# Second phase of a gated cross-attention kernel: who writes its constants and who issues the loads of its MLP weights

## The chip, the cores and the metric

The kernel runs on one core of a Trainium2 chip. The core has TensorE (PE in the profile) for matrix products, VectorE (DVE), ScalarE (ACT), GpSimd (POOL) and SyncE (SP), which issues the DMAs. The metric is the device time of one execution in microseconds; several executions are taken and their median stands for the kernel. One further execution is recorded by the profiler, and every row below comes from that one.

## The reference

The input x is 32 batches of 256 rows by 256 columns; a context of the same size and a mask of 256 by 256 per batch go with it. Four gated residual steps follow each other:

```python
x = x + jnp.tanh(g_xattn[0]) * _L0_xattn_ref(_layernorm(x, axis=-1), ctx_1024, ctx_1024, ...)
x = x + jnp.tanh(g_ffn[0]) * _L0_ffn_ref(_layernorm(x, axis=-1), L0_ffn_weight, L0_ffn_bias)
x = x + jnp.tanh(g_xattn[1]) * _L1_xattn_ref(_layernorm(x, axis=-1), ctx_1024, ctx_1024, mask_Bx1xSxS2_if1, ...)
x = x + jnp.tanh(g_ffn[1]) * _L1_ffn_ref(_layernorm(x, axis=-1), ...)
```

The first phase of the kernel computes the first line. The second line needs one scale over the whole of x (an fp8 quantisation with `quant_fp8`), so the second phase can only start when the first is through. The second phase computes the last three lines: the quantised product, an attention with 16 heads of 16 columns, and an MLP whose weights are dequantised on the chip:

```python
w = (q.astype(jnp.float32) - 128.0).reshape(K // g, g, N) * scales[:, None, :]   # g = 128
y = hf @ w1 + fc1_bias      # 256 -> 1024, then silu
z = y @ w2 + fc2_bias       # 1024 -> 256
```

## The kernel before

x stays in SBUF through both phases. The second phase, `phase_b`, is a pipeline over the 32 batches that is written out by hand for each engine. `iteration(half, parity)` is one step of it, and iteration k works on eight stages at once: n (batch k) is scaled and rounded for the fp8 product, f (batch k-1) gets the product and its update of X, q (k-2) the projections to queries, keys and values, m (k-3) the maxima of the scores, a (k-4) the exponentials and the product with V, o (k-5) the output projection, h (k-6) the first half of the MLP, w (k-7) its second half. Each engine has its own list of calls for an iteration and runs it in that order; semaphores with names (`sig["y"]`, `sig["ones_set"]`) bind the engines together. The first ten iterations and the last seven or so are written out, those between are a loop. Whether a piece of work stands in an iteration is decided by `if n:`, `if f:` and so on, and for work that happens once by `at_iteration(half, parity, k)`.

Around the change:

- Batch 0 goes through VectorE's `scaled`, `binades`, `magic` (tiles `v`, `e`), GpSimd's `rounded` (`v` at L1200, `y` at L1204), four transposing loads on SyncE (`yT<-y`, L1118), TensorE's quantised product (L1736), and VectorE's `quantised_update`: `ob` at L1471 and X at L1475. GpSimd may write `y` of the next batch only when the loads of the last have landed.
- Constants are written once by GpSimd at the end of its iteration 0: 1.0 into both buffers of V (whose columns 16 to 31 of each head sum the exponentials), 0.0 into `nm` (the maxima, of which the transposing load also takes columns that nobody fills), 1.0 into both buffers of K4 (the stacked keys, of which one row multiplies the row of maxima). Five increments of `ones_set` tell the others.
- The tiles Y and YT of the MLP, 1 MB each, also serve as the landing place of the quantised weights and their scales: `load_weights` puts the integers into Y and the scales, repeated over the partitions, into YT. SyncE issues this for fc1 at the end of iteration 0 and for fc2 at the end of iteration 4, then behind waits for `f1lo` and `b1_mm`, which say that fc1 has been taken out.
- VectorE dequantises fc1 at the end of iteration 2 (L1424, L1426), ScalarE and VectorE split it into a bf16 part and a rest in iteration 3 (`f1`), and TensorE multiplies YT with the beta column (`first_bias`, L1671) there. fc2 goes the same way at the end of iteration 5 (`f2`).
- On SyncE iteration 4 ends with the transposed maxima (L1127) and the row of maxima that is laid into Q4 (L1135). TensorE's first transposed score of iteration 5 waits for that row, and ScalarE's first exponential of iteration 5 for this score.
- `load_functions` is a table load of ScalarE, two in every iteration (L31).

Of the kernel before, what the change touches and what calls it, by code (L numbers as in the profile page):

```python
# [6 lines left out]
ALU = mybir.AluOpType  # L7
# [4 lines left out]
P = 128  # L12
D = 256
C = D // P
# [909 lines left out]
def phase_b(nc, a, NB, out_d, ctxT_d, mask_d, X, mu1, rsq, scale_qk, gate, ident, identb, minus_half, f1, f2, b1f, any_masked,  # L924
# [15 lines left out]
    with scope:  # L940
# [227 lines left out]
        def _(pool):  # L1168
# [6 lines left out]
            def iteration(half, parity):  # L1175
# [99 lines left out]
        def _(act):  # L1275
            def iteration(half, parity):
# [70 lines left out]

                if q:
                    normalised_high()
# [33 lines left out]

                if at_iteration(half, parity, 3):

                    act.wait_ge(sig["w1"], 1)
                    for c in range(C):
                        last = nc.scalar.activation(f1[:, 0, c], whole_YT[:, c * HID:(c + 1) * HID], ACT.Copy,
                                                    scale=second["g_col"][:, c:c + 1])
                    last.then_inc(sig["f1hi"], 1)  # L1390
                if at_iteration(half, parity, 5):

                    act.wait_ge(sig["w2"], 1)
                    nc.scalar.activation(f2[:, 0].rearrange("p h d -> p (h d)"), whole_YT, ACT.Copy).then_inc(sig["f2hi"], 1)

# [3 lines left out]
        def _(dve):  # L1399
# [28 lines left out]
            def iteration(half, parity):  # L1428
# [138 lines left out]
                if at_iteration(half, parity, 4):  # L1567

                    dve.wait_ge(sig["b1_mm"], 1)
                    nc.vector.tensor_tensor(b1f[:, :], second["b1_raw"][:, :], b1_ps, ALU.add).then_inc(sig["b1f"], 1)  # L1570
                if h:
                    mlp_normalised()
# [48 lines left out]

                if at_iteration(half, parity, 2):
                    dequantised("f1_in", "w1")
                if at_iteration(half, parity, 3):

                    dve.wait_ge(sig["f1hi"], 1)
                    for c in range(C):
                        last = nc.vector.scalar_tensor_tensor(f1[:, 1, c], whole_YT[:, c * HID:(c + 1) * HID],
                                                              second["g_col"][:, c:c + 1], f1[:, 0, c], ALU.mult,
                                                              ALU.subtract)  # L1630
                    last.then_inc(sig["f1lo"], 1)
# [304 lines left out]
```

## Time and profile before

| what | us |
|---|---|
| median of 3 runs | 1703.47 |
| lowest and highest | 1703.34, 1705.59 |
| the profiled execution | 1701.08 |
| its span, first to last instruction | 1699.2 |
| TensorE busy in it | 1555.5 (92%) |
| VectorE busy | 1369.5 (81%) |
| ScalarE busy | 1045.2 (62%) |
| GpSimd busy | 941.0 (55%) |

Times in the trace are counted from the start of the span. The second phase starts at about 675; its filling lasts until about 830, the loop and its ends from there. A row of the timeline gives the start, the length, the engine, the line of the kernel, the operation and its tiles; in brackets stands how long the engine had been idle before it and what ended that. Rows that follow each other in equal form are merged, with their count. Busy shares are means over stages with different limits, so a place is judged by the chain of work there and not by the share.

### The profile page before, as it was taken

To read this page: it belongs to the slowest core of one execution; us is meant where nothing else is said; L and a number is where in the kernel's file an instruction comes from. 1 tells how busy PE (TensorE), PEld (TensorE's weight loads), DVE (VectorE), ACT (ScalarE), POOL (GpSimd) and SP (SyncE) were. 2 spreads that over 40 slices of the span, in tenths; PEclk is the share of its full clock that TensorE was granted. 3 is DMA by queue.
4 is the path that set the end of the run, shared out by engine and by line. 5 is a ranking of instruction groups with operands and counts; after the bars stand their busy time and mean duration, and the time that the engine had idled before them with its cause. 6 is when DMAs were issued, how large, how long until landed. Compare 5 with 4: busy or idle time off the path is not lost.

```text
span 1699.2 us, 40740 instructions
## 1 busy us (share of the span) xinstructions
PE 1555.5 (92%) x13387; PEld 1206.5 (71%) x13387; DVE 1369.5 (81%) x3213; ACT 1045.2 (62%) x1894; POOL 941.0 (55%) x1328
## 2 busy tenths in 40 slices
PE   5999999999999995376999999999999999999987
PEld 4888888888888884243667766676767676767666
DVE  5688888888888776777899989899888988898743
ACT  6666666666666654245666666666665657575654
POOL 4555556665566534424465656565655656564535
PEclk9999999999999998568999999999999999999999
DMA  7312221222221100323222323232232322222100
GB/s 217 103 63 62 73 82 62 62 62 64 86 66 62 37 1 29 92 81 115 76 82 76 90 73 87 71 86 77 78 85 74 88 74 82 80 80 81 56 16 20
DMA packets 197687, 125.40 MB, mean 74 GB/s; under 512 B 44400, under 2 KB 196848, under 8 KB 197360
## 3 DMA queue, kind: packets, MB, share of 16 engines
q1 hardware_dynamic: 197616, 124.48, 25.0%
q8 instruction: 42, 0.69, 0.2%
q14 instruction: 29, 0.24, 0.0%
HBM read 92.69 MB, written 25.17 MB: 69 GB/s over the span
## 4 chain that ended last, share of the span: by engine, by line
PE 38%; ACT 7%; issue 5%; DVE 3%; SPq 3%; DMA 2%; POOL 1%; ACTq 0%; POOLq 0%
PE b_bank L1646 22%; PE b_bank L1721 6%; PE b_scoreT L1703 4%; PE b_score L1686 3%; ACT L31 2%; ACT b_E L1284 2%; ACT b_Y L1344 2%; PE b_bank L1654 1%; DMA b_nmT<-b_nm 1%; DVE b_nm L1466 1%; PE b_bank L1736 1%; ACT b_xT L1290 1%; DMA b_Q<-b_nmT 1%; SPq L1102 1%; SPq L1091 1%
## 5 line engine op out<-in xcount | busy, mean ns | idle before, releaser
L1466 DVE TENSOR_REDUCE b_nm<-b_score 128x4 bf16<-128x1024 f32 x256 | 314.3, 1228 | 73.4 <-PE b_score L1686 73.2
L1284 ACT ACTIVATE b_E<-b_scoreT 128x1024 f32<-128x1024 f32 x256 | 262.5, 1025 | 156.0 <-PE b_scoreT L1703 155.6
L760 PE MATMUL bank<-W2T,G 128*128 128x256 f32 x1024 | 231.2, 379 | 0.0
L1213 POOL TENSOR_SCALAR b_YT<-b_Y 128x512 bf16<-128x512 f32 x128 | 85.7, 669 | 248.5 <-ACT b_Y L1344 240.2
L760 PEld LDWEIGHTS bank<-W2T,G 128*128 128x128 f32 x1024 | 192.1, 190 | 24.8
L31 ACT ACT_TABLE_LOAD x156 | 200.1, 1283 | 9.7 <-PEq L875 6.4
L1344 ACT ACTIVATE b_Y<-b_bank,b1f 128x256 f32<-128x256 f32 x256 | 107.3, 470 | 158.8 <-PE b_bank L1646 158.4
L1646 PE MATMUL b_bank<-b_hT,f 128*128 128x256 bf16 x1536 | 188.7, 273 | 11.2 <-ACT b_Y L1344 10.9
L1646 PE MATMUL b_bank<-f,b_YT 128*128 128x256 bf16 x1536 | 183.5, 273 | 2.5 <-POOL b_YT L1216 1.6
L727 PE MATMUL bank<-hT,W1T 128*128 128x256 bf16 x1536 | 178.3, 273 | 6.2 <-ACT G L497 2.5
L1646 PEld LDWEIGHTS b_bank<-b_hT,f 128*128 128x128 bf16 x1536 | 142.8, 98 | 54.0 <-ACT b_Y L1344 19.2
L727 PEld LDWEIGHTS bank<-hT,W1T 128*128 128x128 bf16 x1536 | 147.8, 98 | 34.6 <-ACT G L497 15.9
L1646 PEld LDWEIGHTS b_bank<-f,b_YT 128*128 128x128 bf16 x1536 | 145.1, 98 | 31.9 <-issue 12.9
L1216 POOL TENSOR_TENSOR b_YT<-b_Y,b_YT 128x512 bf16<-128x512 f32 x128 | 148.0, 1156 | 10.7
L1721 PE MATMUL b_bank<-b_E,b_V 128*32 128x256 f32 x2048 | 132.5, 388 | 0.0
L497 ACT ACTIVATE G<-bank,b1c 128x256 f32<-128x256 f32 x256 | 103.2, 466 | 46.0 <-PE bank L727 46.0
L1703 PE MATMUL b_scoreT<-b_Q,b_K 49*128 49x256 bf16 x1024 | 101.2, 276 | 28.4 <-ACT b_E L1284 18.7
L1686 PE MATMUL b_score<-b_K,b_Q 48*128 48x256 bf16 x1024 | 101.4, 277 | 16.7 <-DVE b_nm L1466 15.6
L1721 PEld LDWEIGHTS b_bank<-b_E,b_V 128*32 128x32 f32 x2048 | 57.3, 110 | 49.4 <-issue 22.6
L346 POOL TENSOR_SCALAR ve<-mv 128x2 f32<-128x2 f32 x32 | 6.9, 215 | 148.5 <-issue 143.5
L454 ACT ACTIVATE E<-bank,low 128x256 f32<-128x256 f32 x64 | 29.7, 469 | 93.9 <-DVE low L569 93.9
L1703 PEld LDWEIGHTS b_scoreT<-b_Q,b_K 49*128 49x128 bf16 x1024 | 33.3, 95 | 74.9 <-ACT b_E L1284 29.5
(206 smaller groups left out, 3378.9 us busy)
## 6 DMA issues: line engine op xcount, KB each, us to landing
b_Q<-q_dram SPq DMA_DIRECT2D x192, 64.0 KB, 2.5
b_K<-k_dram SPq DMA_DIRECT2D x192, 64.0 KB, 2.5
xin<-in_x SPq DMA_DIRECT2D x32, 256.0 KB, 4.3
ctxn<-in_ctx SPq DMA_DIRECT2D x32, 256.0 KB, 2.8
mask_in<-in_mask SPq DMA_DIRECT2D x32, 256.0 KB, 3.0
X<-in_x SPq DMA_DIRECT2D x32, 256.0 KB, 4.1
ctxt<-in_ctxT SPq DMA_DIRECT2D x32, 256.0 KB, 4.4
b_ctxt<-in_ctxT SPq DMA_DIRECT2D x32, 256.0 KB, 2.8
```

The lines of the kernel that those rows point to most:

```text
L31: act.add_instruction(mybir.InstLoadActFuncSet(name=nc.get_next_instruction_name(), act_func_set_id=which, ins=[], outs=[]))
L497: last = nc.scalar.activation(G[m.parity][:, 2 * j + i], mlp_ps[j % 2][:, i], ACT.Gelu, bias=b1c[:, 2 * j + i:2 * j + i + 1])
L727: last = nc.tensor.matmul(out_tile, lhs(i, k), rhs(j, k), start=k == 0 and (i, j) == TERMS[0], stop=k == chunks[-1] and (i, j) == TERMS[-1])
L760: last = nc.tensor.matmul(out_ps[:, t], G[w.parity][:, h, t * P:(t + 1) * P], W2T[:, h], start=h == 0, stop=h == HC - 1)
L1216: nc.gpsimd.tensor_tensor(YT[:, 1, 2 * j:2 * j + 2], Y[:, 2 * j:2 * j + 2], YT[:, 0, 2 * j:2 * j + 2], ALU.subtract).then_inc(sig["Ylo"], 1)
L1284: nc.scalar.activation(E[:, pair:pair + 2], scoreT_ps[:, :, :, :], ACT.Exp).then_inc(sig["E"], 1)
L1344: last = nc.scalar.activation(Y[:, 2 * j + i], bank[BANK[f"H{j}"]][:, i], ACT.Silu, bias=b1f[:, 2 * j + i:2 * j + i + 1])
L1466: nc.vector.tensor_reduce(pair, score_ps[:, :, :, :], AX.X, ALU.max, negate=True).then_inc(sig["nm"], 1)
L1646: last = nc.tensor.matmul(out_tile, lhs(i, k), rhs(j, k), start=start and k == chunks[0] and (i, j) == TERMS[0], stop=stop and k == chunks ...
L1686: last = nc.tensor.matmul(score_ps[:, odd, t], Q4[m.parity][rows, i, tile(t)], K4[m.parity][rows, i, :], start=True, stop=not mask)
L1703: last = nc.tensor.matmul(scoreT_ps[:, odd, k], K4[a.parity][rows, i, tile(k)], Q4[a.parity][rows, i, :], start=True, stop=not mask)
L1721: last = nc.tensor.matmul(bank[BANK[name]][ONE * j:ONE * (j + 1), g % 2, :], V[a.parity][:, k, i, :], E[:, i % RING, k, :], start=k == 0, ...
```

## The change

GpSimd no longer writes the constants; ScalarE writes them at the end of its iteration 0 with ACTIVATE Copy (input times 0.0 plus the value, `ident` as an input of one column that is repeated). `load_weights` moves from SyncE to ScalarE, for fc1 behind those constants, for fc2 at the end of ScalarE's iteration 4 behind the same two waits. The splitting of `f1` and `f2` on ScalarE and VectorE is put into functions (`weights_high`, `weights_low`) and called at the same places; `first_bias` asks for its iteration itself.

```diff
         @block.sync
         def _(sp):
-            def load_weights(ints, layout, rows, scales, step):
-                sp.dma_start(whole_Y.bitcast(I32).rearrange("p (c o) -> p c o", c=rows),
-                             a[ints].rearrange(layout, p=P)).then_inc(sig[step], 16)
-                sp.dma_start(whole_YT, a[scales].to_broadcast([P, HC * S])).then_inc(sig[step], 16)
-
...
-                if at_iteration(half, parity, 0):
-                    load_weights("fc1_q", "(c p) o -> p c o", C, "fc1_scales", "f1_in")
-                if at_iteration(half, parity, 4):
-
-                    sp.wait_ge(sig["f1lo"], 1)
-                    sp.wait_ge(sig["b1_mm"], 1)
-                    load_weights("fc2_q", "(c p) o -> p c o", HC, "fc2_scales", "f2_in")
...
-                if at_iteration(half, parity, 0):
-                    nc.gpsimd.memset(V[0][:, :, :, :], 1.0).then_inc(sig["ones_set"], 1)
-                    nc.gpsimd.memset(V[1][:, :, :, :], 1.0).then_inc(sig["ones_set"], 1)
-                    nc.gpsimd.memset(nm[:, :, :], 0.0).then_inc(sig["ones_set"], 1)
-                    for i in range(2):
-                        nc.gpsimd.memset(K4[i][:, :, :], 1.0).then_inc(sig["ones_set"], 1)
...
         @block.scalar
         def _(act):
+            def load_weights(ints, layout, rows, scales, step):
+                act.dma_start(whole_Y.bitcast(I32).rearrange("p (c o) -> p c o", c=rows),
+                             a[ints].rearrange(layout, p=P)).then_inc(sig[step], 16)
+                act.dma_start(whole_YT, a[scales].to_broadcast([P, HC * S])).then_inc(sig[step], 16)
...
+                def weights_high():
+                    if at_iteration(half, parity, 0):
+                        for tensor, value in ((V[0], 1.0), (V[1], 1.0), (nm, 0.0), (K4[0], 1.0), (K4[1], 1.0)):
+                            whole = tensor.ap()
+                            nc.scalar.activation(whole, ident[:, 0:1].to_broadcast(list(whole.shape)), ACT.Copy, scale=0.0,
+                                                 bias=value).then_inc(sig["ones_set"], 1)
+                        load_weights("fc1_q", "(c p) o -> p c o", C, "fc1_scales", "f1_in")
...
+                    if at_iteration(half, parity, 4):
+
+                        act.wait_ge(sig["f1lo"], 1)
+                        act.wait_ge(sig["b1_mm"], 1)
+                        load_weights("fc2_q", "(c p) o -> p c o", HC, "fc2_scales", "f2_in")
```

How the instructions stand now, at the places that matter. GpSimd at the start of the second phase, before (two additions for batch 0, the constants, two for batch 1):

```order
L1173 MEMSET b_pool_fence 128x64
L1200 TENSOR_TENSOR b_v<-b_v,b_e 128x512
L1204 TENSOR_TENSOR b_y<-b_v,b_e 128x512
L1266 MEMSET b_V_0 128x1024
L1267 MEMSET b_V_1 128x1024
L1268 MEMSET b_nm 128x256
L1270 MEMSET b_K4_0 128x2048
L1270 MEMSET b_K4_1 128x2048
L1200 TENSOR_TENSOR b_v<-b_v,b_e 128x512
L1204 TENSOR_TENSOR b_y<-b_v,b_e 128x512
```

GpSimd there with the change:

```order
L1159 MEMSET b_pool_fence 128x64
L1186 TENSOR_TENSOR b_v<-b_v,b_e 128x512
L1190 TENSOR_TENSOR b_y<-b_v,b_e 128x512
L1186 TENSOR_TENSOR b_v<-b_v,b_e 128x512
L1190 TENSOR_TENSOR b_y<-b_v,b_e 128x512
```

The five memsets are gone from between the two batches. ScalarE at the same start, before (the table loads of iterations 0 and 1, then iteration 2):

```order
L31 ACT_TABLE_LOAD x4
L1290 ACTIVATE b_xT<-b_bank9 128x512
L31 ACT_TABLE_LOAD
L1303 ACTIVATE b_qs<-b_bank8,bq_col 128x256 x2
L1311 ACTIVATE b_ks<-b_bank6,bk_col 128x256 x2
```

ScalarE there with the change:

```order
L1335 ACTIVATE b_K4_0<-ident 128x2048
L1335 ACTIVATE b_K4_1<-ident 128x2048
L1255 DMA b_Y<-in_fc1_q 128x2x1024
L1257 DMA b_YT<-in_fc1_scales 128x2048
L31 ACT_TABLE_LOAD x2
L1273 ACTIVATE b_xT<-b_bank9 128x512
```

The fills (of which the last two are shown) and the two loads of fc1 now stand between the second and the third table load. SyncE at the end of iteration 4 and the start of iteration 5, before:

```order
L1127 DMA_TRANSPOSE b_nmT_1<-b_nm 128x128 x2
L1135 DMA b_Q4_1<-b_nmT_1 1x8x256 x2
L1051 DMA b_Y<-in_fc2_q 128x8x256
L1053 DMA b_YT<-in_fc2_scales 128x2048
L1062 DMA b_ctxt<-in_ctxT 128x2x256
L1069 DMA b_mask_in<-in_mask 128x2x256
L1118 DMA_TRANSPOSE b_yT<-b_y 128x128 x4
```

ScalarE at the same place with the change (exponentials of iteration 4, its copies, then iteration 5):

```order
L31 ACT_TABLE_LOAD
L1307 ACTIVATE b_oS<-b_bank9 128x512
L1316 ACTIVATE b_V_0<-b_bank6 128x16x16 x2
L1255 DMA b_Y<-in_fc2_q 128x8x256
L1257 DMA b_YT<-in_fc2_scales 128x2048
L1273 ACTIVATE b_xT<-b_bank9 128x512
L31 ACT_TABLE_LOAD
```

The two loads of fc2 have gone from behind the row of maxima on SyncE to between the copies of V and of xT on ScalarE.

## Rows read from the trace of the kernel before

**Rows 1.** stages: PE, PEld, DVE, ACT, POOL busy; clock, DMA share, GB/s

```profile
686.00:709.00 23.00, 8.67 (x48) 5.80 (x48) 14.51 (x33) 5.50 (x9) 10.40 (x12) 0.65 0.27 77
...
860.00:1610.00 750.00, 727.24 (x7706) 522.12 (x7706) 662.81 (x1283) 483.14 (x755) 442.55 (x569) 1.00 0.28 79
```

**Rows 2.** the chain that ended last, 683 to 690: start, length, what

```profile
683.53 2.38 DMA b_yT<-b_y
...
687.95 1.84 DVE X L1475
```

**Rows 3.** line L1475: shortest/median/longest ns, all batches

```profile
L1475 DVE SCALAR_TENSOR_TENSOR X<-b_ob,gate,X x32: 750/752/1844, 687.9 to 1563.0; 128x512 bf16 x22, 128x512 f32<-128x512 bf16 x10
```

**Rows 4.** timeline of GpSimd, start of the second phase

```profile
681.62 3.55 POOL L1270 MEMSET b_K<- 128x2048 bf16 x2
686.64 1.27 POOL L1200 TENSOR_TENSOR b_v<-b_v,b_e 128x512 f32<-128x512 f32 x1 [1.47 <-DVE b_e L1547]
687.98 1.26 POOL L1204 TENSOR_TENSOR b_y<-b_v,b_e 128x512 bf16<-128x512 f32 x1
```

**Rows 5.** timeline of VectorE: v of batches 1 and 2, dequantising fc1

```profile
679.68 5.95 DVE L1529 TENSOR_SCALAR b_v<-X,mu,rsq 128x256 f32<-128x256 f32 x2 [2.79 <-POOL b_y L1204]
...
694.09 0.73 DVE L1529 TENSOR_SCALAR b_v<-X,mu,rsq 128x256 f32<-128x256 f32 x2
...
709.12 1.75 DVE L1424 TENSOR_SCALAR b_Y<-b_Y 128x2048 f32<-128x2048 int32 x1
```

**Rows 6.** the chain that ended last, 762 to 770

```profile
763.59 2.36 DMA b_nmT<-b_nm
...
766.78 1.75 DMA b_Q<-b_nmT
```

**Rows 7.** timeline of ScalarE, iteration 4 to 5

```profile
766.13 0.66 ACT L1333 ACTIVATE b_V<-b_bank 128x256 f32<-128x256 f32 x2 [1.64 <-PE b_bank L1646]
766.67 0.61 ACT L1290 ACTIVATE b_xT<-b_bank 128x512 bf16<-128x512 f32 x1
767.29 1.28 ACT L31 ACT_TABLE_LOAD   x1
769.01 1.02 ACT L1284 ACTIVATE b_E<-b_scoreT 128x1024 f32<-128x1024 f32 x1 [0.43 <-PE b_scoreT L1703]
```

**Rows 8.** timeline of SyncE's queue: fc1, transposing loads, fc2

```profile
675.60 0.46 SPq L1053 DMA_DIRECT2D b_YT<-in_fc_scales  x1
...
679.75 5.02 SPq L1118 DMA_TRANSPOSE b_yT<-b_y  x4
...
767.52 0.41 SPq L1051 DMA_DIRECT2D b_Y<-in_fc_q  x1
767.97 1.54 SPq L1053 DMA_DIRECT2D b_YT<-in_fc_scales  x1
```

**Rows 9.** timeline of ScalarE: start of the second phase, and f2

```profile
675.19 5.15 ACT L31 ACT_TABLE_LOAD   x4 [6.41 <-PEq L875]
695.44 0.60 ACT L1290 ACTIVATE b_xT<-b_bank 128x512 bf16<-128x512 f32 x1 [15.10 <-PE b_bank L1654]
...
791.71 1.91 ACT L1394 ACTIVATE f<-b_YT 128x2048 bf16<-128x2048 f32 x1 [3.49 <-DVE b_YT L1426]
```

**Rows 10.** landings: scales; L1118 768 to 780; L1118 675 to 700

```profile
DMA to landing us min/median/max: 7.0/7.4/7.8
...
DMA to landing us min/median/max: 4.2/5.7/7.3
...
DMA to landing us min/median/max: 2.3/2.4/3.9
```

**Rows 11.** timeline of TensorE: twelve matmuls, slow and fast; b1 product

```profile
696.82 2.74 PE L1646 MATMUL b_bank<-b_xT,wqkvo 128*128 128x256 bf16 x12 [1.42 <-DVE b_xT L1433]
...
703.32 1.48 PE L1646 MATMUL b_bank<-wqkvo,b_cT 128*128 128x256 bf16 x12 [1.40 <-DVE b_ks L1504]
...
733.41 6.83 PE L1671 MATMUL b_scoreT<-b_col,b_YT 128*128 128x1 f32 x32
```

More of the change, by code:

```diff
@@ L1346, in silu @@
                     last.then_inc(sig["Y"], 1)
+                def weights_high():
[5 more added lines that the diff above has]
+                        load_weights("fc1_q", "(c p) o -> p c o", C, "fc1_scales", "f1_in")
+                    if at_iteration(half, parity, 3):
+                        act.wait_ge(sig["w1"], 1)
+                        for c in range(C):
+                            last = nc.scalar.activation(f1[:, 0, c], whole_YT[:, c * HID:(c + 1) * HID], ACT.Copy,
+                                                        scale=second["g_col"][:, c:c + 1])
+                        last.then_inc(sig["f1hi"], 1)
+                    if at_iteration(half, parity, 5):
+                        act.wait_ge(sig["w2"], 1)
+                        nc.scalar.activation(f2[:, 0].rearrange("p h d -> p (h d)"), whole_YT, ACT.Copy).then_inc(sig["f2hi"], 1)
+                    if at_iteration(half, parity, 4):
+                        act.wait_ge(sig["f1lo"], 1)
+                        act.wait_ge(sig["b1_mm"], 1)
+                        load_weights("fc2_q", "(c p) o -> p c o", HC, "fc2_scales", "f2_in")
                 if q:
@@ L1382, in iteration @@
                     silu(3)
[L1384 to L1394, printed above, removed]
+                weights_high()
             pipeline(act, iteration, NB, LAGS)
@@ L1570, in iteration, with weights_low @@
                     nc.vector.tensor_tensor(b1f[:, :], second["b1_raw"][:, :], b1_ps, ALU.add).then_inc(sig["b1f"], 1)
+                def weights_low():
+                    if at_iteration(half, parity, 2):
+                        dequantised("f1_in", "w1")
+                    if at_iteration(half, parity, 3):
+                        dve.wait_ge(sig["f1hi"], 1)
+                        for c in range(C):
+                            last = nc.vector.scalar_tensor_tensor(f1[:, 1, c], whole_YT[:, c * HID:(c + 1) * HID],
+                                                                  second["g_col"][:, c:c + 1], f1[:, 0, c], ALU.mult,
+                                                                  ALU.subtract)
+                        last.then_inc(sig["f1lo"], 1)
+                    if at_iteration(half, parity, 5):
+                        dequantised("f2_in", "w2")
+                        dve.wait_ge(sig["f2hi"], 1)
+                        nc.vector.tensor_tensor(f2[:, 1].rearrange("p h d -> p (h d)"), whole_YT,
+                                                f2[:, 0].rearrange("p h d -> p (h d)"), ALU.subtract).then_inc(sig["f2lo"], 1)
                 if h:
@@ L1620, in iteration @@
                     base()
[L1622 to L1631, printed above, removed]
-                if at_iteration(half, parity, 5):
-                    dequantised("f2_in", "w2")
-                    dve.wait_ge(sig["f2hi"], 1)
-                    nc.vector.tensor_tensor(f2[:, 1].rearrange("p h d -> p (h d)"), whole_YT,
-                                            f2[:, 0].rearrange("p h d -> p (h d)"), ALU.subtract).then_inc(sig["f2lo"], 1)
+                weights_low()
             pipeline(dve, iteration, NB, LAGS)
@@ L1666, in first_bias @@
                 def first_bias():
+                    if not at_iteration(half, parity, 3):
+                        return
                     pe.wait_ge(sig["w1"], 1)
@@ L1882, in iteration @@
                     hidden(3)
-                if at_iteration(half, parity, 3):
-                    first_bias()
+                first_bias()
             some = pe.value_load(any_masked[0:1, 0:1], min_val=0, max_val=1)
```

## The prediction, as it was put on record

> **What bounds the kernel now.** I read the view by stages first. In the 750 us from 860 to 1610 TensorE is busy for 727.24 us at full clock; in the 23 us from 686 to 709, in which the second phase starts, it is busy for 8.67 us, at 0.65 of full clock [rows 1]. The change touches nothing in the stage that repeats. Its instructions all stand in iterations 0 and 4 of the filling, written out ahead of the loop. So nothing is multiplied by 32, and what it can be worth is read from the chain that ended last, at two places.
>
> First place, the chain from 683 to 690 [rows 2]: the fourth transposing load of y for batch 0 takes from 683.53 to 685.91, TensorE makes the quantised product, VectorE `ob`, and then VectorE takes 1.84 us for X at L1475, from 687.95. That last row is strange: over all 32 batches the same line takes 0.750 at least, 0.752 in the median and 1.844 at most [rows 3]. The reader is to see why in GpSimd's rows [rows 4]. Right behind y of batch 0 stand five memsets, of which the last two take 3.55 us from 681.62, up to 685.17. VectorE's `v` for batch 1, issued at 679.68, stays open for 5.95 us [rows 5], until 685.63, and GpSimd's additions for batch 1, which wait for VectorE, run at 686.64 and 687.98, about 1.26 us each, so that the second lies on top of the 1.84 us instruction. The striking 5.95 us are not on the chain: what is late there is the transposing load.
>
> Second place, the chain from 762 to 769: transposed maxima (2.36 us of DMA), the row of maxima laid into Q4 (1.75 us of DMA), the transposed scores, and ScalarE's first exponential of iteration 5 at 769.01 [rows 6, 7]. The load of fc2 is issued behind this, at 767.52 [rows 8].
>
> **The change part by part.**
>
> *Constants leave GpSimd.* The five memsets go. `v` of batch 1 is done some 5.2 us sooner (5.95 against the 0.73 us of batch 2 [rows 5]). GpSimd's `v` addition follows at about 681.3. Its `y` addition has to wait until `yT` of batch 0 has landed, 685.91 [rows 2], and so ends at about 687.2. `ob` hangs on TensorE's product and X starts at 687.95 as before: by then GpSimd is idle, waiting for VectorE's statistics. Term A is 1.84 - 0.75 = **-1.09 us**, on the chain. What comes behind (statistics, GpSimd's power, `xh`, TensorE's transposes, ScalarE's copy) is one chain in which each waits for the one before, so the whole filling moves by that much. The ends of this term are 0 and -1.09.
>
> *Constants go to ScalarE.* It loads four tables from 675.19 for 5.15 us and then does nothing until 695.44, idle for 15.10 us [rows 9]. The new work stands between the second and the third table load. A fill of 128x2048 to bf16 goes by the nearest row, 1.91 us for f2 [rows 9]: two of these, two of half the size, one of an eighth, together 2 x 1.91 + 2 x 0.96 + 0.24 = about 6 us. ScalarE is free again at about 675.2 + 5.15 + 6 = 686.3, plus 0.9 us of issue, 687.2, against a need at about 694.4 (695.44 less term A). That costs nothing; it begins to cost if the fills take over twice as long. Those who wait for the constants (SyncE before it stacks the keys of batch 0, ScalarE itself before V, VectorE before its first maximum, behind the row at 709.12 [rows 5]) come more than 10 us later. Also nothing.
>
> *The load of fc1 moves.* It is 2 MB; on SyncE its second half is issued at 675.60 in 0.46 us and lands 7.0 to 7.8 us after its issue [rows 8, 10]. VectorE takes it at 709.12 [rows 5]. Even issued behind the fills, at 683.8, it lands by 692. Hidden, with 17 us to spare. But it may fall on the transposing loads of `yT` (issued from 679.75 for 5.02 us [rows 8]), and those are on the chain. Of the eight such loads from 675 to 700 the median lands after 2.4 us and the slowest, beside the burst of fc1 itself, after 3.9 us; behind the burst of fc2 they take 4.2 to 7.3 us [rows 10]. Term B lies between 0 and 7.3 - 2.4 = +4.9 us. I take **0**: if ScalarE issues it early, the burst ends near 683.4 as it does now; if it issues it behind the fills, at 683.8, three of the four loads are through. Only a start between 679 and 682 is bad.
>
> *The load of fc2 moves.* SyncE is rid of 0.41 + 1.54 us at 767.52 [rows 8]; its next loads start up to 1.95 us sooner and nobody is waiting for them. ScalarE gets the two issues between the copy of V (766.13, for which it had been idle 1.64 us) and the copy of `xT` at 766.67, behind which stand a table load (767.29 to 768.57) and the exponential at 769.01 [rows 7]. No row shows an issue from ScalarE; the nearest are SyncE's. If it comes in its turn, ScalarE loses 1.95 us, of which the 0.44 us between the table and the exponential cover a part: +1.51 us on the chain, through TensorE's second transposed score and all that follows it. If the queue issues it while the engine waits for V, it is covered but for 1.95 - 1.64 = 0.31 us. Term C is 0 to +1.51; I take **+0.31**, because the later of the two waits in front of the issue, `b1_mm`, was met at 740.24 [rows 11], and ahead of it stands only work of the engine that waits for TensorE. The page that bears on this is in the Trainium skill, Perfetto Trace Analysis, "Per-engine timelines": an instruction of ScalarE goes to a wait queue and the sequencer decodes on. By it term C would be 0 or 0.31, and fc1 would be issued as early as now. No run here shows it.
>
> VectorE's and TensorE's edits only put the same instructions into functions; their order stays.
>
> **The sum.** -1.09 + 0 + 0 + 0.31 = -0.78 us. The profiled execution took 1701.08 us (span 1699.2): it would take 1700.3. That execution lies 2.39 us below the median of the three runs; the difference is carried over to the median: 1703.47 - 0.78 = **1702.7 us**. The 0.2% that a measurement of this kernel can tell from no change is 3.4 us.
>
> **The rivals.**
>
> *In its turn* (chance 0.2). ScalarE issues fc2 only behind V: -1.09 + 1.51 = +0.4, 1703.9 us. For it: order in the program. Against it: nothing that the trace can show.
>
> *The burst falls on the chain* (0.18), the one that ends slower. If ScalarE's queue can issue fc2 while the engine waits, the 2 MB start two or more us sooner, beside the transposed maxima and the row of maxima (2.36 and 1.75 us [rows 6]). Beside a burst the same kind of transfer took 1.8 to 4.9 us more. That gives -1.09 + 1.8 = +0.7 up to -1.09 + 4.9 = +3.8, 1704.2 to 1707.3 us. It is slower than before as soon as the delay exceeds 1.1 us, and measurably slower from 4.5 us. Against it: in [rows 10] the loads stood behind the burst in one queue, here they would be in two. The rule against the change is in the Trainium skill, DMA: Bandwidth & Descriptors, "Issuing engines are not separate DMA queues": a DMA issued from ScalarE runs on the same 16 engines and interleaves, and only issue time is saved. By that the move gains nothing and a delay above 0 is to be expected. The same mechanism at term B has the same prices.
>
> *The change doesn't relieve the chain* (0.1). The 1.84 us of L1475 has another cause than GpSimd, or `yT` lands so that GpSimd's `y` falls on it again: A is 0, 1703.5 to 1704.3 us. The one length in 32 and the overlap speak against it.
>
> *TensorE's clock shifts* (0.12). From 686 to 709 it is granted 0.65 of full speed [rows 1]; twelve matmuls take 2.74 us at 1.2 GHz and 1.48 us at 2.4 GHz, both on this path [rows 11]. A shift of all work by 1 us can move a few such groups from one level to the other: 1.26 us each, one to three of them, either way: 1699 to 1707 us.
>
> **How the numbers follow.** The forecast has 0.4. Its own range is -1.4 to +0.5 around the median. The range for 8 in 10 takes in the rival in its turn, most of the burst, one or two groups of matmuls and what executions of one kernel differ by (2.39 us down, 2.12 us up): 1700.6 to 1706.5. Faster by over 0.2% would take two or three groups at the better clock besides term A: 0.05, all from the clock. Slower by over 0.2% needs the burst near its upper end (0.04) or the clock (0.02). Within: 0.89.
>
> **What would show it.** Right: L1475's longest is near 0.75 us; `v` of batch 1 takes 0.7 us; ScalarE's issues of fc2 leave `xT` on time; all marks of the filling up to 766 are 1.1 us earlier. Wrong: `yT` or the row of maxima land later; a gap of 2 us on ScalarE at the end of iteration 4; another clock in 686 to 740.

## The result and the profile after

The changed kernel takes 1713.26 us in the median (1707.32 to 1715.89, five runs), the kernel before beside it 1704.52 (1703.34 to 1705.59, five runs). The ratio is 1.0049, with a 95% interval of 1.0028 to 1.0071: slower by some 0.5%, where 1702.7 (1700.6 to 1706.5) had been forecast. The profiled execution of the changed kernel took 1707.32 us (span 1705.5), that of before 1701.08 (span 1699.2), so the two traces show 6.3 us of the difference.

The stage that repeats is the same (727.74 us of TensorE against 727.24 in [rows 1]). The stages of the filling are not. Stages of the changed kernel, columns as in [rows 1]:

```profile
686.00:709.00 23.00, 8.76 (x48) 5.87 (x48) 13.19 (x32) 5.72 (x10) 9.42 (x12) 0.65 0.27 78
...
740.00:772.00 32.00, 21.27 (x184) 10.80 (x183) 20.76 (x38) 16.32 (x21) 6.77 (x8) 0.76 0.36 109
...
860.00:1610.00 750.00, 727.74 (x7705) 522.96 (x7703) 663.95 (x1283) 483.48 (x758) 443.51 (x569) 1.00 0.28 80
```

To find where the time went I take marks in both traces, relative to VectorE's first instruction of the second phase (675.23 before, 675.19 after):

| mark, us from the start of the phase | before | after | difference |
|---|---|---|---|
| TensorE's quantised product of batch 0 | 10.73 | 11.52 | +0.79 |
| X of batch 0 starts | 12.72 | 13.50 | +0.78 |
| VectorE's `xT` of batch 0 (L1433 before) | 20.84 | 20.54 | -0.30 |
| TensorE's b1 product | 58.18 | 57.96 | -0.22 |
| first transposed score of iteration 5 | 93.35 | 97.88 | +4.53 |
| TensorE's transposes of `hn` | 122.19 | 128.82 | +6.63 |
| first result of the phase | 175.40 | 181.89 | +6.49 |
| end of the span | 1023.97 | 1030.31 | +6.34 |

The loss arises between the b1 product and the transposes of `hn` and stays to the end.

**First place.** The chain that ended last, changed kernel, 683 to 690, answering to [rows 2] (start, length, what):

```profile
683.49 3.17 DMA b_yT<-b_y
...
688.69 0.75 DVE X L1470
```

X takes 0.75 us, as forecast, and the longest of the 32 is now 753 ns, where [rows 3] had 1844. But `yT` lands 3.17 us after its last issue instead of 2.38. ScalarE's timeline in the changed kernel shows why (ACT is the engine, ACTq its queue, which issues the DMAs); it answers to [rows 9] and to the first row of [rows 8]:

```profile
675.15 2.57 ACT L31 ACT_TABLE_LOAD   x2 [6.41 <-PEq L875]
677.73 1.05 ACT L1335 ACTIVATE b_V<-ident 128x1024 f32<-128x1024 f32 x1
677.74 0.45 ACTq L1255 DMA_DIRECT2D b_Y<-in_fc_q  x1
678.23 0.48 ACTq L1257 DMA_DIRECT2D b_YT<-in_fc_scales  x1
...
679.94 3.69 ACT L1335 ACTIVATE b_K<-ident 128x2048 bf16<-128x2048 f32 x2
683.65 2.57 ACT L31 ACT_TABLE_LOAD   x2
```

In the program the load of fc1 stands behind the five fills. The queue issues it at 677.74, when the engine has just begun the first of them, but not ahead of the two table loads, which end at 677.72. So the 2 MB start 2.6 us later than before and are still moving when the transposing loads go out.

**Second place.** ScalarE from iteration 4 to 5 in the changed kernel, answering to [rows 7]:

```profile
765.89 0.38 ACT L1316 ACTIVATE b_V<-b_bank 128x256 f32<-128x256 f32 x1 [1.64 <-PE b_bank L1642]
765.96 0.39 ACTq L1255 DMA_DIRECT2D b_Y<-in_fc_q  x1
...
766.37 0.61 ACTq L1257 DMA_DIRECT2D b_YT<-in_fc_scales  x1
767.08 0.60 ACT L1273 ACTIVATE b_xT<-b_bank 128x512 bf16<-128x512 f32 x1 [0.53 <-issue]
...
773.72 1.02 ACT L1267 ACTIVATE b_E<-b_scoreT 128x1024 f32<-128x1024 f32 x1 [4.74 <-PE b_scoreT L1700]
```

The issue itself is cheap: two instructions, 0.39 and 0.61 us, and ScalarE waits 0.53 us for its queue ahead of `xT`, at 767.08 against 766.67. The queue issued fc2 0.07 us after the first copy of V had begun (765.89); it did not do so in the 1.64 us for which the engine had waited for that copy. The exponential comes 4.71 us later (773.72 against 769.01) for another reason, which the chain that ended last shows, answering to [rows 6]:

```profile
764.08 2.38 DMA b_nmT<-b_nm
...
767.29 5.73 DMA b_Q<-b_nmT
...
773.07 0.63 PE b_scoreT L1700 x3
```

SyncE's row of maxima, two pieces of 4 KB, takes 5.73 us from its issue where it took 1.75. fc2 was issued 0.6 us ahead of it (765.96 against 766.55), by another queue, where SyncE had issued it 1.5 us behind it (767.52 against 766.04, [rows 8]). TensorE's rows, and its granted clock in steps of 1 us, both of the changed kernel:

```profile
773.07 0.60 PE L1700 MATMUL b_scoreT<-b_Q,b_K 49*128 49x256 bf16 x4 [5.48 <-DMA b_Q<-b_nmT]
...
775.76 2.74 PE L1642 MATMUL b_bank<-b_xT,wqkvo 128*128 128x256 bf16 x12
...
780.52 1.48 PE L1642 MATMUL b_bank<-b_cT,wqkvo 128*128 128x256 bf16 x12
```

```profile
771.00:772.00 1.00, 0.00 (x0) 0.00 (x0) 0.00 (x0) 0.00 (x0) 0.00 (x0) 1.00 1.01 417
772.00:773.00 1.00, 0.00 (x0) 0.00 (x0) 0.00 (x0) 0.00 (x0) 0.00 (x0) 0.56 1.01 413
773.00:774.00 1.00, 0.93 (x6) 0.53 (x7) 0.00 (x0) 0.28 (x1) 0.00 (x0) 0.50 0.91 321
```

TensorE stands still for 5.48 us; in the gap its clock falls from full speed to half of it (2.4 to 1.2 GHz), while the DMA engines move over 400 GB/s. The twelve matmuls that follow take 2.74 us; in the kernel before the same twelve took 1.48, at 770.64. The loss adds up: the row was issued 0.55 us later (the first transposing load of the maxima took SyncE 1.84 us against 1.11), it travelled 3.98 us longer, together 4.53; and by 780.52 the half clock had added another 2.1 (+6.64 there; 105.33 against 98.69 us from the start of the phase).

### The profile page after: what moved, and what is told of

Read it like the earlier page. It is cut to its first block, busy times and chain, and to the rows that moved or that the text cites. A ratio compares the mean times of both kernels' runs of the same rounds, so it can differ in the third digit from the quotient of the medians.

```text
span 1705.5 us, 40740 instructions
## 1 busy us (share of the span) xinstructions
PE 1557.9 (91%) x13387; PEld 1207.2 (71%) x13387; DVE 1362.1 (80%) x3213; ACT 1051.1 (62%) x1899; POOL 935.7 (55%) x1323
## 4 chain that ended last, share of the span: by engine, by line
PE 38%; ACT 7%; issue 5%; DVE 4%; DMA 3%; SPq 2%; POOL 1%; ACTq 0%; POOLq 0%
PE b_bank L1642 22%; PE b_bank L1718 6%; PE b_scoreT L1700 4%; PE b_score L1683 3%; ACT L31 2%; ACT b_E L1267 2%; ACT b_Y L1327 2%; DVE b_nm L1461 1%; PE b_bank L1650 1%; DMA b_nmT<-b_nm 1%; DMA b_Q<-b_nmT 1%; PE b_bank L1733 1%; ACT b_xT L1273 1%; SPq L1122 1%; SPq L1097 1%
```

## The experiments

The theory after the result: fc2, started ahead of the row of maxima by another queue, holds the row up (some 4 us), and the gap costs TensorE its clock (some 2 us more). Rivals: ScalarE's time is the cost; the load of fc1 or the constants are; the traffic slows all work beside it. The mark that tells most is the first result of the phase, since what comes after differs between executions of one kernel (below). "Late" is counted against the profiled execution of before, from the start of the phase; each kernel has one profile, the change two.

**Only fc2 back on SyncE.** From the changed kernel:

```diff
 # SyncE, end of iteration 4
+                if at_iteration(half, parity, 4):
+                    sp.wait_ge(sig["f1lo"], 1)
+                    sp.wait_ge(sig["b1_mm"], 1)
+                    load_weights("fc2_q", "(c p) o -> p c o", HC, "fc2_scales", "f2_in")
 # ScalarE, weights_high
-                    if at_iteration(half, parity, 4):
-                        act.wait_ge(sig["f1lo"], 1)
-                        act.wait_ge(sig["b1_mm"], 1)
-                        load_weights("fc2_q", "(c p) o -> p c o", HC, "fc2_scales", "f2_in")
```

> The change with the load of fc2 back at the end of SyncE's iteration 4; constants and fc1 stay on ScalarE. Theory (the 2 MB of fc2, issued from ScalarE ahead of the row of maxima, hold that row for 5.73 instead of 1.75 us, and TensorE's clock falls in the gap): the row lands after 1.75 us again and the time is that of before, from 1.1 us less (L1475) to 0.8 us more (yT beside fc1), in the profile about 0.3 us less. Rival (the constants and fc1 at the start, which shift all work and so the clock, make the loss): still 6 to 9 us slower than before.

Measured: 1703.13 us against 1704.26, ratio 0.9993 (0.9980 to 1.0006). The row of maxima takes 1.75 us again, the first result is 0.4 us late. In its chain at the start `yT` and X read much as in the changed kernel:

```profile
681.86 3.06 DMA b_yT<-b_y
...
686.95 0.75 DVE X L1475
```

So the whole measurable loss goes with the place of fc2. The load of fc1 on ScalarE's queue costs 0.7 us at the landing of `yT` and the constants give 1.09 back.

**Only fc2 on ScalarE,** everything else as in the kernel before:

```diff
 # SyncE, end of iteration 4: the block with load_weights of fc2 is gone
 # ScalarE, end of iteration 4
+                if at_iteration(half, parity, 4):
+                    act.wait_ge(sig["f1lo"], 1)
+                    act.wait_ge(sig["b1_mm"], 1)
+                    load_weights("fc2_q", "(c p) o -> p c o", HC, "fc2_scales", "f2_in")
```

> The kernel before with only the load of fc2 moved, to the end of ScalarE's iteration 4. Theory (burst on the row of maxima): 6 to 9 us slower than before, the row lands after 5 us or more, VectorE's L1475 keeps its 1.84 us. Rival (the loss needs the constants and fc1): within 1.5 us of before.

Measured: 1708.64 us, ratio 1.0024 (1.0009 to 1.0039). The start of the phase is that of before, X at L1475's place keeps its 1.84 us, and the row of maxima is held up as in the change:

```profile
766.08 5.70 DMA b_Q<-b_nmT
...
771.83 0.63 PE b_scoreT L1708 x4
```

The first transposed score is 5.04 us late, the first result 6.32. One part alone makes the loss of the filling. Its median is 4.4 us above that of before, less than the 6 to 9 us expected.

**Only the constants on ScalarE.** Both loads stay on SyncE; the ACTIVATEs of the change write the constants.

```diff
 # GpSimd, end of iteration 0: the five memsets are gone
 # ScalarE, weights_high
+                    if at_iteration(half, parity, 0):
+                        for tensor, value in ((V[0], 1.0), (V[1], 1.0), (nm, 0.0), (K4[0], 1.0), (K4[1], 1.0)):
+                            whole = tensor.ap()
+                            nc.scalar.activation(whole, ident[:, 0:1].to_broadcast(list(whole.shape)), ACT.Copy, scale=0.0,
+                                                 bias=value).then_inc(sig["ones_set"], 1)
```

> Only the constants on ScalarE, both loads on SyncE. Term A by itself: 1.1 us less than before in the profile, X of batch 0 in 0.75 us, yT of batch 0 landed 2.4 us after its issue as before; in the times 0 to 1.1 us less, which is inside what executions differ by. Rival: as slow as the change.

Measured: 1703.68 us, ratio 0.9999 (0.9981 to 1.0017). At the start of its second phase the chain reads:

```profile
681.77 2.39 DMA b_yT<-b_y
...
686.19 0.75 DVE X L1476
```

`xT` of batch 0 comes at 19.75 us, 1.09 sooner than before: term A to the hundredth. At the b1 product 0.20 of it is left, and the profiled execution as a whole is not 1.1 us shorter, as had been expected, but as long as that of before (1701.22 against 1701.08). TensorE's rows of iteration 2, first of this kernel and then of the kernel before:

```profile
693.97 2.74 PE L1648 MATMUL b_bank<-b_xT,wqkvo 128*128 128x256 bf16 x12 [1.41 <-DVE b_xT L1434]
696.50 2.57 PE L1648 MATMUL b_bank<-b_cT,wqkvo 128*128 128x256 bf16 x12
```

```profile
699.35 2.13 PE L1646 MATMUL b_bank<-b_cT,wqkvo 128*128 128x256 bf16 x12
```

The first twelve take 2.74 in both [rows 11]; of the second twelve, fewer run at the full clock when the work comes sooner, 2.57 against 2.13. Counted from the start of the phase the second twelve start at 23.0 us here and at 24.1 in the kernel before, but the clock rises at 25.3 and at 25.4. From 709 to 740 the mean granted clock is 0.56 in this kernel and 0.61 in the kernel before. The work came sooner, the time at which the clock stood at its higher level hardly did. The two groups account for 0.44 of the 0.89 us lost by the b1 product; the rest was not followed.

**The change again,** unaltered, beside these.

> The change, unaltered, again. Its five executions went from 1707 to 1716 us and the profiled one was the fastest. Theory: executions differ in how much of the burst stands ahead of the row and in how long TensorE is slow after the gap; 3 to 12 us above before, at a mean granted clock lower the slower they are, and the row of maxima late in each profile. Rival (one odd first series): all within 1 us of before.

Measured: 1711.94 us (twelve runs), ratio 1.0040 (1.0027 to 1.0052). Row of maxima 5.87 us, first result 6.43 late. In more executions the result stands; the two shortest had a mean granted clock of 0.968, the longest 0.962.

**fc2 on ScalarE, but behind the row.** From the changed kernel: the four lines of fc2 go out of `weights_high` and stand between the two first exponentials of iteration 5.

```diff
                 if a:
                     exponential(0)
+                if at_iteration(half, parity, 5):
+                    act.wait_ge(sig["f1lo"], 1)
+                    act.wait_ge(sig["b1_mm"], 1)
+                    load_weights("fc2_q", "(c p) o -> p c o", HC, "fc2_scales", "f2_in")
+                if a:
                     exponential(1)
```

> The change with the load of fc2 still issued by ScalarE, but behind the first exponential of iteration 5, which cannot start before the row of maxima has landed. Theory (what costs is the place of the burst ahead of the row, not the queue that issues it): the row lands 1.75 us after its issue, the first transposed score of iteration 5 comes about 94 us after the start of the second phase as in the kernel before (93.35) and with fc2 on SyncE (94.20), and the time is within 2 us of before. Rival (an issue or a burst from ScalarE's queue costs wherever it stands): 4 us or more above before, ScalarE's second exponential late by 1 us or more.

Measured: 1705.52 us against 1702.74, ratio 1.0016 (0.9998 to 1.0034). ScalarE's timeline:

```profile
770.83 1.02 ACT L1267 ACTIVATE b_E<-b_scoreT 128x1024 f32<-128x1024 f32 x1 [1.48 <-PE b_scoreT L1700]
770.89 0.42 ACTq L1255 DMA_DIRECT2D b_Y<-in_fc_q  x1
771.34 0.64 ACTq L1257 DMA_DIRECT2D b_YT<-in_fc_scales  x1
772.34 1.03 ACT L1267 ACTIVATE b_E<-b_scoreT 128x1024 f32<-128x1024 f32 x1 [0.49 <-PE b_scoreT L1700]
```

The two issues lie under the first exponential, and the next one waits for TensorE, as it does before. The first transposed score is 0.32 us late, the first result 0.11 early. The same queue, engine and bytes cost nothing here: the loss is neither ScalarE's time nor ScalarE's queue, it is the order. The median is 2.8 us above the one of before, where at most 2 had been expected, with an interval that just takes in 1; the filling doesn't show these 2.8, so this stays open.

**fc2 ahead of the row, but on SyncE.** From the kernel before; ScalarE has no part in it.

```diff
 # SyncE, end of iteration 4
                     transpose_maxima()
+                    if at_iteration(half, parity, 4):
+                        sp.wait_ge(sig["f1lo"], 1)
+                        sp.wait_ge(sig["b1_mm"], 1)
+                        load_weights("fc2_q", "(c p) o -> p c o", HC, "fc2_scales", "f2_in")
                     row_of_maxima()
 # ... and the block behind it is gone
```

> The kernel before with the load of fc2 on SyncE, but between the transposed maxima and the row of maxima. Theory (the row stands behind the burst in the DMA engines, whichever queue issued it): the row lands 5 us or more after its issue, TensorE's first transposed score of iteration 5 is 4 to 6 us late, the whole 5 to 12 us slower. Rival (only a second queue disturbs the first): the row lands after 1.75 us, the time is that of before.

Measured: 1713.52 us (one run). Row of maxima on the chain:

```profile
766.41 6.34 DMA b_Q<-b_nmT
...
772.80 0.63 PE b_scoreT L1702 x3
```

Here with one queue 6.34 us, there with two 5.70 to 5.87. First result 6.98 late. But here fc2 had a longer start on the row (issued at 764.41, the row at 765.68, so 1.27 us against 0.59 to 1.05). Counted from the issue of fc2 the row lands after 8.34 us here and after 7.06 to 7.49 with two queues; here 0.4 us behind the scales of fc2, there 0.8 to 1.2 ahead of them. A second queue saves the row 0.9 to 1.3 us of the wait behind 2 MB, not the wait. This is one profile of the one-queue kernel.

**Half of fc2 ahead of the row.** From the kernel before, 1 MB on ScalarE at the end of iteration 4, the other half on SyncE behind the row: once the integers, once the scales.

```diff
 # the one with the integers on ScalarE
+                if at_iteration(half, parity, 4):
+                    act.wait_ge(sig["f1lo"], 1)
+                    act.wait_ge(sig["b1_mm"], 1)
+                    act.dma_start(whole_Y.bitcast(I32).rearrange("p (c o) -> p c o", c=HC),
+                                 tensors["fc2_q"].rearrange("(c p) o -> p c o", p=P)).then_inc(sig["f2_in"], 16)
 # SyncE, in the place of load_weights
+                    sp.dma_start(whole_YT, tensors["fc2_scales"].to_broadcast([P, HC * S])).then_inc(sig["f2_in"], 16)
```

> The kernel before, with the integers of fc2 (1 MB) issued by ScalarE at the end of iteration 4 and the scales (1 MB) by SyncE behind the row of maxima. Theory (the row waits for what is queued ahead of it): about half of the delay, the row lands 3 to 4.5 us after its issue instead of 5.7, the first transposed score of iteration 5 at 95 to 97 us after the start of the phase. Rival (any issue from ScalarE costs the same): 5.7 us as with both halves.

> As the run before, the halves exchanged: the scales (1 MB, one row of 8 KB repeated over the partitions) from ScalarE, the integers from SyncE behind the row. Theory (bytes ahead count): again 3 to 4.5 us. If the form of the transfer counts (long rows against 1 KB pieces), the two halves differ by over 1 us.

Measured: 1710.74 and 1707.32 us (one run each). The row of maxima on the two chains, first with the integers ahead, then with the scales:

```profile
767.01 4.48 DMA b_Q<-b_nmT
```

```profile
764.50 4.18 DMA b_Q<-b_nmT
```

Against 1.75 that is 2.73 and 2.43 us more for 1 MB, 3.95 to 4.12 for 2 MB on the second queue. The rearranged integers and the repeated scales differ little. The other half was issued 0.7 us behind the row, while the row was still moving; what it added isn't separated. With one issue in place of two ScalarE's `xT` is not delayed (0.60 and 0.55 us behind V, 0.54 before). Half the bytes don't save half of the loss: the first result is 6.55 and 5.71 us late. That asked for an experiment in which the row is late and nothing is in its way.

**A late row without traffic.** The kernel before; SyncE counts up a semaphore that nobody waits for, 40 or 80 times, between the landing of the maxima and the issue of their row, in iteration 4 alone. All loads keep queue and order.

```diff
+                    if at_iteration(half, parity, 4):
+                        for _ in range(40):          # 80 in the second
+                            sp.sem_inc(sig["row_late"], 1)
                     sp.sem_inc(sig["row_ready"], 1)
```

> The kernel before with SyncE made to count up a semaphore that nobody waits for 40 times between the landing of the maxima and the issue of the row of them, in iteration 4 alone; all loads in their old places and queues, so no burst stands ahead of the row. It asks what a late row costs without the traffic. At 0.05 us for each count (the steps between two issues of SyncE in the trace of before are 0.04 to 0.06 us) the row is issued 2 us later. Theory (only the lateness of the row costs, and what is beyond it is TensorE's clock after the longer gap): row 1.75 us from issue to landing, first transposed score 2 us later, and the first result by more than that, 3 to 6 us, as in the run with the scales alone on ScalarE's queue (2.3 us late, 5.7 us at the first result). Rival (the traffic beside the work costs the rest): the first result is late by the same 2 us or less.

> The same with 80 counts, the row issued 4 us later, as late as it landed in the changed kernel. Theory: row 1.75 us from issue to landing, first transposed score 4 to 5 us later, TensorE's clock falls in the gap as in the changed kernel, and the first result is 6 to 7 us late, the time 1709 to 1713. Rival (the burst itself slows the work): the first result is late by 4 us or less, the time 1706 to 1708. A third one: SyncE's loads behind the row (fc2, the context and the transposing loads of batch 1) go out 4 us later too, and cost something of their own; then yT of batch 1 is what ends the wait for the next MLP, and the loss is over 7 us.

Measured: with 40 counts 1712.46 us (one run), with 80 counts 1710.29 us (ten runs), ratio 1.0030 (1.0014 to 1.0047). Chain and stages of the kernel with 40:

```profile
771.84 1.76 DMA b_Q<-b_nmT
...
773.64 0.63 PE b_scoreT L1706 x3
```

```profile
768.00:772.00 4.00, 0.98 (x8) 0.54 (x8) 2.84 (x5) 1.75 (x2) 2.79 (x4) 1.00 0.01 2
772.00:776.00 4.00, 2.29 (x16) 1.28 (x16) 0.64 (x3) 1.02 (x1) 0.00 (x0) 0.69 0.50 152
```

The DMA engines move next to nothing (2 GB/s) from 768 to 772, the row needs its 1.76 us, and the clock falls to half all the same (0.50 from 774 to 775, behind a wait of 4.63 us that ended at 773.64). The row went out later than I had put (3.10 and 5.82 us, for 2 and 4): the counts took some 2.9 and 5.2 us, and in both kernels the transposing load of the maxima took SyncE 2.1 us instead of 1.11. The first result is 6.15 and 7.18 us late, as in the kernels with a burst. The rival in which traffic slows the work beside it falls. The third one had a loss of over 7 us as its sign, and 7.18 just meets it; but the late row accounts for it as in the others (5.84 at the score, 1.42 added by the transposes of `hn`, nothing after), and up to the first result TensorE's longer waits are for the same work as in the changed kernel.

Put together, lateness of the first transposed score of iteration 5, of the transposes of `hn` and of the first result, one profile each:

| kernel | score late | `hn` late | first result late |
|---|---|---|---|
| only the constants | -0.19 | -0.19 | -0.56 |
| fc2 on ScalarE behind the row | 0.32 | 0.50 | -0.11 |
| fc2 back on SyncE | 0.85 | 0.85 | 0.41 |
| fc1 first on ScalarE (below) | 1.22 | 2.78 | 2.90 |
| scales ahead | 2.31 | 3.81 | 5.71 |
| 40 counts | 3.12 | 5.60 | 6.15 |
| integers ahead | 3.75 | 6.29 | 6.55 |
| the change | 4.53 | 6.63 | 6.49 |
| the change again | 4.82 | 6.80 | 6.43 |
| only fc2 on ScalarE | 5.04 | 6.95 | 6.32 |
| fc2 ahead, on SyncE | 5.55 | 7.26 | 6.98 |
| 80 counts | 5.84 | 7.26 | 7.18 |

In the first three kernels the clock stays at full speed around the first scores of iteration 5, and by `hn` at most 0.2 us is added to the lateness (in two of them it falls for some 3 us about 12 us later, at no cost that this mark shows). In the other nine profiles it falls to half in the gap or just behind it, for 3 to 7 us, and 1.4 to 2.5 us are added. So the price is the lateness itself plus some 2 us for the clock, and the second part hardly depends on the first. The last column flattens for another reason too: with the scales ahead another 1.9 us are lost behind `hn`, where the clock is at half again (0.50 from 832 to 834, 1.00 there in the kernel before); why isn't shown.

**fc1 first on ScalarE,** the version meant to keep the gain: constants on ScalarE, fc2 on SyncE at its old place, fc1 issued by ScalarE as the first thing of its iteration 0, ahead of the table loads.

```diff
+                if at_iteration(half, parity, 0):
+                    load_weights("fc1_q", "(c p) o -> p c o", C, "fc1_scales", "f1_in")
                 if q:
                     normalised_high()
```

> The version meant to keep the gain and drop the losses: the constants stay on ScalarE, fc1 is issued by ScalarE as the first thing of its iteration 0, ahead of its table loads and fills, and fc2 goes back to the end of SyncE's iteration 4. Theory (fc1 costs only where it overtakes the transposing loads of batch 0, and fc2 only where it overtakes the row of maxima): yT of batch 0 depends on how far ahead of it fc1 starts. In the change fc1 started 2.5 us behind the start of the phase and yT took 3.17 us; before, it was issued behind yT and yT took 2.38. Started at the very beginning, the 2 MB have moved for most of their 7 us by the time yT is issued, so 2.4 to 4 us for yT; row of maxima 1.75 us; first result within 1 us of the kernel before; time 1702 to 1705 against 1704.3 of before, not to be told from it. Rival (a load on a second queue always delays the chain that runs beside it, and an earlier start only moves the place): yT is 1 to 4 us later than before, and the end 1 to 4 us later, 1705 to 1708.

Measured: 1704.11 us against 1704.58, ratio 0.9997 (0.9981 to 1.0014). ScalarE and the chain at the start of the phase:

```profile
675.71 0.46 ACTq L1265 DMA_DIRECT2D b_Y<-in_fc_q  x1
676.21 0.48 ACTq L1267 DMA_DIRECT2D b_YT<-in_fc_scales  x1
676.72 2.57 ACT L31 ACT_TABLE_LOAD   x2 [7.42 <-issue]
```

```profile
684.06 2.40 DMA b_yT<-b_y
...
688.49 0.75 DVE X L1476
```

Issued 2 us sooner than in the change, fc1 is out of the way, and `yT` lands after 2.40 us. (The expectation has it that the kernel before issued fc1 behind `yT`; [rows 8] has it at 675.6 and `yT` at 679.75. This version gives fc1 its old moment back, so it does not test an earlier one.) `xT` of batch 0 comes 1.06 sooner, and again nothing of it reaches the end. Its profiled execution happened to be a long one (1712.24): the transposing load of the maxima took SyncE 2.41 us instead of 1.11, which made the row 1.22 late with no load near it, and the result 2.90, where within 1 had been expected. TensorE's clock fell behind this wait too, to 0.50 from 773 to 774; its rows show the wait and the twelve matmuls behind it, which took 1.48 us in the kernel before:

```profile
770.32 0.39 PE L1706 MATMUL b_scoreT<-b_Q,b_K 49*128 49x256 bf16 x4 [2.06 <-DMA b_Q<-b_nmT]
...
772.38 2.36 PE L1648 MATMUL b_bank<-b_xT,wqkvo 128*128 128x256 bf16 x12
```

None of the kernels beats the one before by an amount that can be told.

## Why the prediction was wrong, point by point

**What bounds the kernel now** held: the repeating stage is untouched, and the two places that I read were the two that moved.

**Term A (-1.09)** was right in mechanism and size where it acts (X 0.75, `xT` of batch 0 at -1.09 with the constants alone). Wrong was "the whole filling moves by that much": by the b1 product 0.20 was left, and about half of what was lost is seen in slower matmuls. It was a gain of a start, in a stretch in which the clock sets how long TensorE's part takes. The fills took 5.9 us (677.73 to 683.63) against 6 forecast, hidden as argued.

**Term B (0)** fell between the two ends: +0.7 to +0.8. I reasoned "if ScalarE issues it early, the burst ends near 683.4 as it does now". The queue passed the fills but not the table loads, so early meant 2.6 us later than before, and the burst ended near 685.5. I had written that only a start between 679 and 682 is bad; one at 677.7 was enough.

**Term C (+0.31) is the step that failed.** In the sum it priced the *issue* and put the *transfer* at nothing. The price of the issue came out near (`xT` 0.41 us later in the trace, 0.65 us later behind V: 1.19 against 0.54), but partly by luck. I had the two issues take 1.95 us and hide in the 1.64 us for which the engine waits for V; they took 1.00 us, came only after that wait, and hid in part under the copies. The sentence "the later of the two waits in front of the issue was met at 740.24" said already that fc2 would leave as soon as ScalarE's queue got to it, at about 766.0, 1.5 us sooner than before and so ahead of the row of maxima instead of behind it. From there it follows from [rows 10]: loads behind the burst of fc2 had landed after 4.2 to 7.3 us. The true term was +3.98 for the row, inside the 1.8 to 4.9 of the rival, and that rival, which had 0.18, is what happened. The argument against it, two queues instead of one, was worth about 1 us: in two queues the row landed 7.06 to 7.49 us after the issue of fc2, in one 8.34. The Trainium skill, DMA: Bandwidth & Descriptors, "Issuing engines are not separate DMA queues", says that DMAs of different engines interleave on the same 16 engines; the runs agree with it, and I should have given it the weight of the sum and not of a rival.

**The clock rival (0.12) and the burst rival were not rivals** but one case. I had the clock as noise that comes "either way" from a shift of 1 us; what it did was follow from a gap of 5.5 us, and add 2.1 us. Lateness of the score 4.53 (the 0.2 left of term A is in it), clock 2.1: 6.6, which is what the profile gives at the transposes of `hn` (6.63; 6.49 at the first result). That GpSimd is not the cause of the 1.84 us is refuted by the rows. fc2 in its turn is refuted in its price (+1.51) and half so in its mechanism: the issue waited with the first copy of V and then went ahead of the second.

**The range** ended at 1706.5 since it took in most of the burst without its follow-up; slower by over 0.2%, which is what came, had 0.06. With the follow-up, the burst's case is 1703.47 + 0.7 to + 3.8, and 2 for the clock: 1706 to 1709. The measured medians, 1711.94 and 1713.26, are higher still, 7.7 and 8.7 us above those of before. What is left beside the 6.4 of the filling, 1.3 and 2.3 us, has no profile that shows its place. The emptying is the likely one, since there executions differ: from the first result to the end of the span the kernel before took 848.6 us in its profile, the kernel with the constants alone 851.1, the change 848.4 and then 854.2, while to X of the last batch it was 712.4 to 713.4 us in all four. From 1640 to 1660, kernel before, and then only fc2 on ScalarE:

```profile
1640.00:1660.00 20.00, 18.71 (x188) 13.68 (x188) 7.12 (x19) 12.44 (x19) 8.40 (x12) 1.00 0.05 15
```

```profile
1640.00:1660.00 20.00, 17.75 (x134) 10.23 (x133) 1.74 (x6) 9.98 (x11) 0.65 (x1) 0.66 0.01 2
```

TensorE is busy for about as long but does 134 matmuls for 188, at 0.66 of its clock. Whether the change makes this more frequent was not settled; single executions of before range from 1697 to 1711 us. Nor was it settled why the whole change is 3.3 us slower in the median than fc2 alone (the intervals, 1.0027 to 1.0052 and 1.0009 to 1.0039, overlap, and the fillings agree within 0.1 us).

## What to carry to other kernels

When a load is moved to another engine's queue, don't price the issue; ask at what moment the queue reaches it now, which small transfer is issued right behind that moment, and who waits for that one. If the answer is TensorE, and the gap grows past what it bridged before, add a clock that falls, here some 2 us. And a gain at the start of a filling is only worth what is left of it once TensorE's clock has risen: read it at a late mark, not where it arises.

## What the runs showed of the hardware

- ScalarE's queue issues a DMA ahead of ACTIVATEs that stand before it in the program and wait for nothing but the engine (fc1 at 677.74, the first fill at 677.73, five of them before it), but it issued none ahead of the table loads from 675.15 to 677.72, nor ahead of an ACTIVATE that waits for TensorE: fc2 came 0.06 to 0.07 us after the first copy of V had begun in all five profiles that have it there, and 0.06 us after the exponential that had waited 1.48 us (770.89 against 770.83).
- The Trainium skill, Perfetto Trace Analysis, "Per-engine timelines", has ScalarE's instructions go to a wait queue, to wait there for their semaphores, while the sequencer decodes on. The fills agree with it. The copy of V and the exponential do not, and the table loads held the queue too. Which of the semaphores in front of the copy and the exponential held it, and whether such a wait is an instruction of its own there, isn't shown.
- Two pieces of 4 KB issued behind a load of 1 MB landed after 4.18 to 4.48 us, behind 2 MB after 5.70 to 5.87 in another queue (which had been issued 0.6 to 1.05 us ahead) and 6.34 in the same (1.3 us ahead), alone after 1.75. During the 2 MB, from 768 to 775 in the change, the DMA engines moved 311 to 433 GB/s.
- TensorE's clock fell from 1.00 to 0.50 in a wait of 5.48 us beside DMA traffic of 311 to 433 GB/s from 768 on, and right behind a wait of 4.63 us beside next to none (2 GB/s from 768 to 772, the kernel with 40 counts). In the nine profiles where it fell at this place, for 3 to 7 us, the lateness grew by 1.4 to 2.5 us up to the transposes of `hn`.
- The first transposing load of the maxima (L1127) takes SyncE between 1.11 and 2.41 us to issue in iteration 4 over the thirteen profiles, 1.11 in three of them; in that place this alone makes up to 1.3 us. What lengthens it isn't shown.
- 40 increments of a semaphore held SyncE for some 2.9 us, 80 for some 5.2: 0.07 us for one, where the steps between two issues are 0.04 to 0.06.
